# Norms and states of block one interleaved with the last two experts, token places ahead of both recurrences, gains applied per slot

## The reference

```python
# block one, end: mixture of 8 experts, all of them for every token
h = relu(einsum('bsd,edf->bsef', x, w1) + b1)
y = einsum('bsef,efd->bsed', h, w2) + b2
x = layernorm(x + einsum('bse,bsed->bsd', probs, y), ln2_g, ln2_b)
...
x = x + s * silu(x_ffn)                      # s: the states of block one
xn = layernorm(x)
# block two: a gated recurrence on 256 channels
h = xn * rsqrt(mean(xn * xn) + EPS) * w_norm
u, z = split(h @ W_in.T); u = silu(u)
lam = sigmoid(u @ W_dt.T + b_dt)
s_t = lam_t * s_{t-1} + (1 - lam_t) * u_t    # scan over the tokens
s = xn + (s * silu(z)) @ W_out.T
# block two: 16 experts, the two likeliest of each token
probs = softmax(xn @ Wr + br); vals, idx = top_k(probs, 2); w = vals / sum(vals)
y = (silu(xn @ W1[e]) * (xn @ W3[e])) @ W2[e]
y = (y - mean) * rsqrt(var + EPS) * gamma[e] + beta[e]
x = x + s * silu(sum over the two of w * y)
```

## Time and profile before

| what | value |
|---|---|
| median of 3 runs | 1208.86 us (1208.67 to 1210.43) |
| the profiled execution: time, span | 1212.35 us, 1210.6 us |
| granted clock of TensorE, mean | 0.955 |
| PE busy | 1129.3 us, 93% |
| DVE, ACT, POOL busy | 915.2 us (76%), 805.2 us (67%), 346.8 us (29%) |
| last expert's last matmul begins | 953.08 us |
| first slot's hidden matmuls begin | 1033.89 us |
| last output op of VectorE ends | 1207.77 us |

### The profile page before, as it was taken

One profiled execution on the slowest core, in us unless ns is written; L12 is line 12 of the kernel. 1 busy time (PEld: TensorE's weight loads), 2 busy tenths in 40 slices (PEclk: granted clock), 3 DMA queues, 4 the chain that ended last, 5 costly groups with the idle time before them and its releaser, 6 DMA issues.

```text
span 1210.6 us, 19401 instructions
## 1 busy us (share of the span) xinstructions
PE 1129.3 (93%) x6417; PEld 471.0 (39%) x6417; DVE 915.2 (76%) x1403; ACT 805.2 (67%) x1490; POOL 346.8 (29%) x860
## 2 busy tenths in 40 slices
PE   5979999999999999999999999999999677899995
PEld 2412222222222222222222345444444353899994
DVE  3589999999999999999999754333334879466665
ACT  2668898888888888888888854333333444255551
POOL 0376653243222342222322110000000011356651
PEclk9779999999999999999999999999999869899995
DMA  3313321032100322102011222100000011467743
GB/s 113 138 28 81 89 72 55 31 94 55 47 29 28 87 60 49 33 32 67 29 31 36 71 80 126 35 18 18 17 17 1 0 36 51 150 210 238 236 130 115
DMA packets 65253, 85.81 MB, mean 71 GB/s; under 512 B 28562, under 2 KB 39834, under 8 KB 64898
## 3 DMA queue, kind: packets, MB, share of 16 engines
q1 hardware_dynamic: 54306, 69.95, 18.3%
q0 software_dynamic: 10208, 13.45, 4.8%
q10 hardware_dynamic: 646, 1.23, 0.3%
HBM read 58.79 MB, written 25.76 MB: 70 GB/s over the span
## 4 chain that ended last, share of the span: by engine, by line
PE 40%; issue 33%; POOL 19%; DVE 7%; ACT 1%; DMA 1%; POOLq 0%; SPq 0%; ACTq 0%; DVEq 0%
PE PS L1691 9%; PE PS L1701 9%; PE PS L1869 7%; POOL neg_m L635 6%; POOL big L449 4%; PE PS L1879 3%; POOL big L467 2%; PE PS L1466 1%; PE PS L1815 1%; DVE mx L1052 1%; POOL m_cols L640 1%; POOL m_cols L642 1%; POOL m_rest L641 1%; POOL m_rest L643 1%; POOL m_cols L644 1%
## 5 line engine op out<-in xcount | busy, mean ns | idle before, releaser
L1052 DVE TENSOR_REDUCE mx<-PS 128x1 f32<-128x1024 f32 x512 | 593.9, 1213 | 21.4 <-PE PS L1538 10.3
L1553 PE MATMUL PS<-big 59*128 59x512 bf16 x1024 | 295.1, 387 | 7.3 <-ACT xnT L812 1.6
L1538 PE MATMUL PS<-big 56*128 56x512 bf16 x1024 | 202.0, 385 | 15.5 <-DVE mx L1052 8.5
L812 ACT ACTIVATE ctx_sb<-PS 128x512 f32<-128x512 f32 x344 | 187.8, 604 | 23.2 <-PE PS L1553 23.2
L812 ACT ACTIVATE xn<-PS 128x512 f32<-128x512 f32 x340 | 185.7, 604 | 26.2 <-PE PS L1553 26.2
L812 ACT ACTIVATE xnT<-PS 128x512 f32<-128x512 f32 x340 | 185.6, 605 | 21.6 <-PE PS L1553 21.6
L1553 PEld LDWEIGHTS PS<-big 59*128 59x128 bf16 x1024 | 72.7, 93 | 323.2 <-ACT ctx_sb L812 98.2
L1182 DVE TENSOR_TENSOR ctx_sb<-big,PS 128x512 f32<-128x512 f32 x128 | 87.9, 687 | 132.2 <-PE PS L1701 78.2
L864 ACT ACTIVATE big<-PS,col_sb 128x512 f32<-128x512 f32 x128 | 87.9, 687 | 133.0 <-PE PS L1691 119.9
L635 POOL TENSOR_SCALAR neg_m<-mx 128x1 f32<-128x1 f32 x256 | 68.6, 287 | 371.6 <-DVE mx L1052 371.6
L1691 PE MATMUL PS<-big,w_bufs 128*128 128x512 f32 x256 | 133.5, 604 | 0.1
(11 more groups left out here) (263 smaller groups left out, 1119.7 us busy)
## 6 DMA issues: line engine op xcount, KB each, us to landing
big<-in_w_in SPq DMA_DIRECT2D x47, 512.0 KB
o_dram<-o_sum SPq DMA_DIRECT2D x64, 256.0 KB, 2.3
big<-parts_dram POOLq DMA_DIRECT2D x42, 128.0 KB, 4.6
w_bufs<-in_w SPq DMA_DIRECT2D x16, 256.0 KB, 2.6
big<-in_w_out SPq DMA_DIRECT2D x2, 2048.0 KB, 11.6
w_bufs<-o_dram SPq DMA_DIRECT2D x3, 1024.0 KB, 5.0
big<-parts_dram SPq DMA_DIRECT2D x62, 48.0 KB
big<-m_dram SPq DMA_DIRECT2D x128, 3.0 KB
```

The source lines that it names most:

```text
L812: nc.scalar.activation(probs[i % SLOTS][:, r, :], PS[:, SB + n % SLOTS, :], ACT.Exp, scale=DH ** -0.5).then_inc(exp_done, 1)
L1052: v.tensor_reduce(mx[:, b % 2, 2 * u + half:2 * u + half + 1], PS[:, MB + 2 * half:MB + 2 * half + 2, :].rearrange("p b n -> p (b n)"), AX ...
L1538: mm = pe.matmul(PS[:, MB + 2 * half + k, :], q_all[rows_of, h, t * P:(t + 1) * P], k_all[rows_of, h, half * CH:(half + 1) * CH], start=Tr ...
L1553: pe.matmul(PS[:, SB + n % SLOTS, :], k_all[rows_of, h, at:at + P], q_all[rows_of, h, qc * CH:(qc + 1) * CH], start=True, stop=True).then_ ...
```

## The change

The last two experts are interleaved chunk by chunk (`LAST_PAIR`: both experts on chunk 0, then both on chunk 1, and so on), so that a chunk's sum is whole two blocks ahead of the next one. Behind it, among the units of the next chunk, stand that chunk's residual, turn, stats, gain, shift, Silu, state product and next norm (`last_act`, `last_dve`, `experts_last`); VectorE reads the turned sum from PSUM, without ScalarE's copy, and gain and shift are fused with mean and root. After the experts only chunk 3 is left, and the turns, logits and first projections of chunks 0 to 2 are queued in its waits. ScalarE scales all 16 tiles; GpSimd scales none. The tokens are placed ahead of both recurrences. In the slots VectorE loads the expert's index into a register and multiplies the output with that expert's row of gains and, with the root, adds its row of shifts; two broadcasts of 16 rows bring these rows to all partitions. In the tail the two rows of a token are only weighted and added (`mix_rows`, `scale_rows`), and SyncE and ScalarE issue half of the reads each. `LAG` lets the last groups of slots be finished sooner.

```diff
 GROUPS = [*(range(i, i + 4) for i in range(0, NT - 3, 4)), range(NT - 3, NT - 1), range(NT - 1, NT)]
+LAG = [2] * (len(GROUPS) - 4) + [1] * 2 + [0] * 2
...
+        gain_rows, shift_rows = big[:, 6 * N:6 * N + E1 * P], big[:, 10 * N + 4 * P:10 * N + 4 * P + E1 * P]
...
+        LAST_PAIR = tuple((e, c) for c in range(C) for e in (E0 - 2, E0 - 1))
...
+        SECOND_MM = Order(("A", 0), ("A", 1), ("A", 2), ("B", 0), ("B", 1), ("U", 0), ("A", 3), ("B", 2), ("L", 0),
+                          ("U", 1), ("U", 2), ("B", 3), ("U", 3), ("K", 0), *(("W", c) for c in range(C)),
+                          *(("M", i) for i in range(2 * C)), ("R", 0), *(("Z", i) for i in range(2 * C)),
+                          *(("Y", c) for c in range(C)))
...
+            sp.wait_ge(ctx_ready, C)
+            sp.dma_start(gain_rows, gains[0].partition_broadcast(P)).then_inc(gains_in, 16)
+            sp.dma_start(shift_rows, gains[1].partition_broadcast(P)).then_inc(gains_in, 16)
...
-            pool.wait_ge(rms_inv, 1)
-            pool.wait_ge(norm3, T)
-            for t in range(T // 2, T):
-                nc.gpsimd.tensor_scalar(hN[:, t, :], xn2[:, t, :], rms[:, t:t + 1], None, ALU.mult)\
-                    .then_inc(h_norm_pool, 1)
...
+            def last_act(i, f):
+                c = i // 2 - 1
+                if c < 0:
+                    return
+                if (i % 2, f) == (0, 0) and c > 0:
+                    root(3, c - 1)
+                elif (i % 2, f) == (0, 3):
+                    root(2, c)
+                elif (i % 2, f) == (1, 1):
+                    silu_sum(c)
+                elif (i % 2, f) == (1, 3) and c == LATE - 1:
+                    root(3, c)
...
+            copy_turned2(0)
+            copy_turned2(1)
+            root(2, LATE)
+            root_means(0)
+            copy_turned2(2)
+            silu_sum(LATE)
+            act.wait_ge(norm3, LATE * TC)
             act.wait_ge(rms_inv, 1)
+            scale_tiles2(0, 2 * TC)
+            gain_turned2(0)
+            root(3, LATE)
+            scale_tiles2(2 * TC, LATE * TC)
+            copy_turned2(LATE)
+            root_means(1)
+            for c in range(1, LATE):
+                gain_turned2(c)
             act.wait_ge(norm3, T)
-            for t in range(T // 2):
-                nc.scalar.activation(hN[:, t, :], xn2[:, t, :], ACT.Copy, scale=rms[:, t:t + 1]).then_inc(h_norm, 1)
+            act.wait_ge(rms_inv, 2)
+            scale_tiles2(LATE * TC, T)
...
+            def gain_sum(c):
+                for i in range(TC):
+                    t = c * TC + i
+                    last = v.scalar_tensor_tensor(x1[:, t, :], summed(c)[:, i, :], moments[:, t, 0:1], row("ln2_g"),
+                                                  ALU.subtract, ALU.mult)
+                    if i < TC - 1:
+                        ch.did(last)
+                last.then_inc(sum_used, 1)
+
+            def shift_sum(c):
+                dve.wait_ge(ln_std, 2 * C + NORMS.n(2, c))
+                ch.step(v.reciprocal(rstd[:, c * TC:(c + 1) * TC], rstd[:, c * TC:(c + 1) * TC]))
+                dve.wait_ge(sum_used, c + 1)
+                for t in range(c * TC, (c + 1) * TC):
+                    v.scalar_tensor_tensor(x1[:, t, :], x1[:, t, :], rstd[:, t:t + 1], row("ln2_b"),
+                                           ALU.mult, ALU.add).then_inc(norm2, 1)
...
+            def last_dve(i, f):
+                c, final = i // 2 - 1, i // 2 == LATE
+                if c < 0:
+                    return
+                if i % 2 == 0:
+                    if f == 0 and c > 0:
+                        third_apply(c - 1)
+                    elif f > 0:
+                        (add_residual, sum_stats, gain_sum)[f - 1](c)
+                elif f == 0:
+                    shift_sum(c)
+                elif f == (1 if final else 2):
+                    add_states(c)
+                elif f == (2 if final else 3):
+                    third_stats(c)
+                elif f == 3:
+                    third_apply(c)
+
+            for i, (e, c) in enumerate(LAST_PAIR):
+                for f in range(FT):
+                    weigh((E0 - 2) * C + i, e, c, f)
+                    last_dve(i, f)
+            add_residual(LATE)
+            mean_squares(0)
+            sum_stats(LATE)
+            gain_sum(LATE)
+            shift_sum(LATE)
+            mean_inverses(0)
+            add_states(LATE)
+            third_stats(LATE)
+            third_apply(LATE)
+            mean_squares(1)
+            mean_inverses(1)
...
-            recur(0)
             name_experts()
             place_tokens()
+            recur(0)
             recur(1)
...
+                e = experts[n] = expert(n)
...
-                v.tensor_copy(y_ring[:, r, :], PS[:, YB + n % 2, 0:P]).then_inc(yt_dve, 1)
-                dve.wait_ge(yt_dve, n + 1)
-                ch.step(v.bn_stats(y_st[:, r, :], y_ring[:, r, :]))
+                y = PS[:, YB + n % 2, 0:P]
+                ch.step(v.bn_stats(y_st[:, r, :], y))
                 ch.step(v.bn_aggr(y_mom[:, r, :], y_st[:, r, :]))
+                v.scalar_tensor_tensor(y_ring[:, r, :], y, y_mom[:, r, 0:1], gain_rows[:, bass.ds(e * P, P)],
+                                       ALU.subtract, ALU.mult).then_inc(yt_dve, 1)
...
+                    e = experts[n]
+                    last = v.scalar_tensor_tensor(y_ring[:, r, :], y_ring[:, r, :], y_rstd[:, r:r + 1],
+                                                  shift_rows[:, bass.ds(e * P, P)], ALU.mult, ALU.add)
                     if n < GROUPS[i][-1]:
                         ch.did(last)
...
+            def mix_rows(c):
+                dve.wait_ge(rows_back[c], 16 * 2)
+                for t in range(c * TC, (c + 1) * TC):
+                    dve.wait_ge(rows_scaled, t + 1)
+                    last = v.scalar_tensor_tensor(y2[:, t, :], y2[:, t, :], wgt[:, 1, t:t + 1], y1[:, t, :],
+                                                  ALU.mult, ALU.add)
+                    if t < (c + 1) * TC - 1:
+                        ch.did(last)
+                ch.settle()
+                last.then_inc(mixed, 1)
+
+            def add_experts(c):
+                dve.wait_ge(silu1, c + 1)
+                ch.step(v.tensor_tensor(chunk(y2, c), chunk(y2, c), chunk(s1, c), ALU.mult))
+                v.tensor_tensor(chunk(x_sb, c), chunk(x_sb, c), chunk(y2, c), ALU.add).then_inc(done, 1)
...
+            def turn_state(c):
+
+                pe.wait_ge(sum_used, c + 1)
+                fill("S", c, turn_tiles(lambda i: sT[:, (c * TC + i) * P:(c * TC + i + 1) * P]))
...
+            def experts_last():
+
+                units, at = len(LAST_PAIR) * FT, (E0 - 2) * C
+                for u in range(units):
+                    n = u + 2
+                    if n < units:
+                        e, c = LAST_PAIR[n // FT]
+                        hidden(at + n // FT, e, e % 2, c, n % FT, E0 // 2)
+                    i, f = u // FT, u % FT
+                    e, c = LAST_PAIR[i]
+                    add_up(at + i, e, e % 2, c, f, E0 // 2, e == E0 - 1)
+                    if i >= 2 and (i % 2, f) == (0, 1):
+                        turn_sum(i // 2 - 1)
+                    if i >= 2 and (i % 2, f) == (1, 0):
+                        turn_state(i // 2 - 1)
...
+            turn_norm(0)
+            turn_norm(1)
+            turn_sum(LATE)
+            logits(0)
+            logits(1)
+            turn_norm(2)
+            logits(2)
+            turn_state(LATE)
+            turn_scaled(0)
+            turn_scaled(1)
...
+                if c == 1:
+                    turn_norm(LATE)
+                    turn_scaled(2)
+                    logits(LATE).then_inc(second_mm, 1)
+                if c == LATE:
+                    turn_scaled(c)
```

331 lines of the change are left out of this document (123 added, 208 removed).

## The result

The changed kernel takes 1190.66 us in the median of 4 runs (1189.66 to 1192.03), the kernel before 1209.2 in 4 runs (1208.67 to 1210.43): a ratio of 0.9846, with an interval from 0.9829 to 0.9863. It is faster, by 18.5 us, and lies inside the forecast range, 3.7 us above the forecast of 1187. The profiled execution of the changed kernel took 1192.03 us with a span of 1190.2; before it was 1212.35 and 1210.6.

What follows compares the result with a forecast made beforehand. TensorE was taken to set the pace, with gains where it waits: behind the experts, before the slots, after the last slot. 13.3 + 3.6 + 5.4 = 22.3 us off the 1208.86 median gave 1187 us, range 1179 to 1198.

Steps and rivals of the forecast that it cites:

- Term 1: Experts' last blocks to the router's softmax sum: interleaving makes the sum start at 974.95 instead of 988.2, 13.3 us gained.
- Term 2: Softmax sum to slot 0: placing tokens ahead of both recurrences makes it 42.0 us instead of 45.65, 3.6 us gained.
- T: The time at which VectorE ends placing the tokens; slot 0 was forecast 11.7 us behind it, before 10.5.
- The bound without the hold, T + 6.4: Earliest slot 0 if recurrence instructions do not delay gathers: 6.4 us behind the placing's end, 2.2 us more gain.
- Slots, nothing: In the slots, VectorE's new register load costs nothing, issued behind the 0.69 us product; slots keep 2.79 us.
- Term 3: Tail after the last slot: VectorE needs 10.6 us for the output instead of 16.0, 5.4 us gained.
- I take the difference off the median: Final sum: the profiled time was 3.5 above the runs' median, so the 22.3 us gain was subtracted from 1208.86.
- the first: Rival, boundary to slot 0: more comes out as the clock stays up or gathers are not held; 1179 to 1183, chance 0.15.
- The second: Rival, slots: VectorE becomes their bound by up to 0.45 us each; 1193 to 1207, chance 0.14.
- the fourth: Rival, slots: the register load holds VectorE for its whole time, making the kernel slower, up to 1215; chance 0.05.
- The third: Rival, last experts: the stall moves into them, overrunning by 6 us; 1190 to 1193, chance 0.08.
- The fifth: Rival, slot 0: token order alone does nothing, its product waiting for the recurrences instead; no separate chance, inside the sum.

Runs made afterwards that it cites:

- e2: Changed kernel with the first recurrence put back ahead of naming the experts and placing the tokens on VectorE: 1195.68 us.
- e3: Changed kernel with two more register loads of the same expert number on VectorE ahead of each slot's output, three in all: 1209.53 us.
- e5: Changed kernel with both recurrences waiting until the third gather has landed: 1194.10 us.
- e6: Changed kernel with the two recurrences cut into sixteen pieces, one in each of the first sixteen slots, and their gating moved later: 1188.97 us.
- e7: Changed kernel with ScalarE's root of the last group of four outputs taken one place later, behind the last slot's Silu: 1189.78 us.
- e9: Changed kernel with both tables of the tail's returning rows read on SyncE's queue alone: 1191.73 us.
- e11: Changed kernel with one more register load of the same expert number on VectorE per slot, two in all: 1194.29 us.

## Why the prediction was right, and where it was off

**Term 1, 13.3 us.** The mechanism and the size were right. The sum came 17.7 us behind the experts' end (forecast 17.95; 17.7 to 18.2 in the other runs that left this stretch alone). From the block that begins at 901.33 in the earlier trace rows to the experts' end it was 52.9 us, and from 905.08 on it is 56.0: the last pair grew by 3.1 us, forecast 2.8. In the first profile the end came at 961.05 and not at 957.0; 3.7 of these 4.1 us are the two losses in untouched code, which came and went in the other profiles. Inside the stretch ScalarE's root came last, as written: it ended 4.58 us behind the end of the Silu (forecast 4.55). What the chain did not have is that VectorE's state product waited for the turned states, 1.04 us beyond the Silu; it cost nothing, because VectorE then still had 0.64 us to wait for the root. Timeline of the changed kernel, ScalarE's Silu and root and then VectorE's state product and norm:

```profile
966.61 0.63 ACT L884 ACTIVATE xn<-xn 128x512 f32<-128x512 f32 x1
...
971.62 0.20 ACT L729 ACTIVATE rstd<-rstd 128x4 f32<-128x4 f32 x1
...
968.28 0.69 DVE L1253 TENSOR_TENSOR xn<-xn,PS 128x512 f32<-128x512 f32 x1 [1.81 <-PE PS L1734]
...
971.86 0.18 DVE L1030 RECIPROCAL rstd<-rstd 128x4 f32<-128x4 f32 x1 [0.64 <-ACT rstd L729]
```

**Term 2, 3.6 us, was 4.9.** T + 11.5 against the T + 11.7 forecast, gathers held as written. What was off in this profile is the clock: I charged 2.8 us to the inner projections, and they lost some 1.6 (from the sum to the slot-finding 25.9 us, before 24.3). In seven other profiles that left this stretch alone (e2, e3, e5, e6, e7, e9, e11) it took 26.7 to 27.2 us, with a clock of 0.86 to 0.88 behind the mask: there 2.4 to 2.9 us were lost, and the charge was about right. So term 2 was 4.9 us in the two profiles of the changed kernel itself and would be some 4 in those. The bound without the hold, T + 6.4, was too early: its own terms make 6.15, and e5 and e6 gave 7.85 and 7.6, because slot 0 then came 3.1 to 3.4 us behind the third gather's end and not 1.85.

**Slots, nothing.** Right that a load behind the product is hidden: no slot of the changed kernel is longer than 2.79 us apart from the start, the states' slots and the last. The row that I took for the price, SyncE's 0.93 with the transfer, was not the nearest: the trace of before has TensorE's own loads of this register at L1854, 0.30 us each in the median, and SyncE's at L588, 0.27. With the register instruction behind it (0.15) that is half of the 0.93 or less, and nearer to the 0.57 that e3 found for a load. But the margin was less than I wrote; one load more cost 5 us. The slots as a whole lost 1.3 us, of which 2.2 is the wait ahead of the last outputs, less a cheaper slot 0 (5.47 instead of 6.37).

**Term 3, 5.4 us, was 7.3.** VectorE's 10.66 us are the forecast 10.6. The rest lies ahead of it: from the last outputs to the first row it was 15.1 us instead of 16.9, as the last seven scatters began 0.24 us behind the last outputs instead of 1.73. I had counted the earlier finish of the last groups as nothing, the gain against the delay. Both were larger than the 1.28 us that I named, but against the wait of 2.2 us, which stands in the slots, they still come to about nothing. No run separates the earlier finish from the rest of the tail.

**The level.** In the profiles the touched stretches gained 13.2 + 4.9 − 1.3 + 7.3 = 24.1 us, the sum said 22.3, and 3.7 were lost elsewhere. That the sum came so near is in part luck: terms 2 and 3 were 1.3 and 1.9 us too small, the slots 1.3 too good. The step that put the forecast 3.7 us below the median is "I take the difference off the median": that median of three runs stood low. Measured again beside the experiments, the kernel before had medians of 1210.2 to 1211.8 over 7 to 17 runs; against 1211.79 the changed kernel's second median, 1189.07, is 22.7 us less, which is the sum. (The intervals of the two ratios, 0.9829 to 0.9863 and 0.9795 to 0.9839, overlap, so 18.5 and 22.7 us are two readings of one gain.) Off the profiled execution's own time the forecast would have been 1190.05.

**The rivals.** Of the first, the gathers that are not held fall by e2 and e5; of its clock, 1.2 of the 2.8 us came between sum and slot-finding, and 0.9 at slot 0. The second and the fourth fall for one load, but their mechanism is real, with 0.57 us for each load that nothing covers. The third falls: the blocks of the last pair took 7.52 us, and the products trailed only at the end (0.45 and 0.87 us). The fifth falls by e2: the order alone is worth some 7 us.
